# GAT softmax denominators: found per edge by segmented scans, and the all-ones product of the first gather pass removed

## The reference

```python
alpha = leaky_relu(a_src[src] + a_dst[dst] + a_edge, 0.2)
amax  = segment_max(alpha, dst)
ex    = exp(alpha - amax[dst])
denom = segment_sum(ex, dst)
w     = ex / (denom[dst] + 1e-16)
out   = segment_sum(h[src] * w[:, None], dst)   # h = x @ W, 128 wide
x     = x + out + bias
```

## Time and profile before

| | before |
|---|---|
| median of 3 runs | 6623.92 us |
| lowest and highest | 6615.25, 6627.57 us |
| span of the profiled execution (no other time is given for it) | 6635.5 us |
| PE, DVE, ACT, POOL busy | 74%, 41%, 17%, 52% |
| mean granted TensorE clock | 0.738 of full speed |
| first gather pass | from 403 to 1381 us of the span |

### The profile page before, as it was taken

One profiled execution on the slowest core, in us unless ns is written; L12 is line 12 of the kernel. 1 busy time (PEld: TensorE's weight loads), 2 busy tenths in 40 slices (PEclk: granted clock), 3 DMA queues, 4 the chain that ended last, 5 costly groups with the idle time before them and its releaser, 6 DMA issues.

```text
span 6635.5 us, 123629 instructions
## 1 busy us (share of the span) xinstructions
PE 4909.3 (74%) x40104; PEld 3977.9 (60%) x40104; DVE 2748.4 (41%) x9007; ACT 1139.0 (17%) x2152; POOL 3474.9 (52%) x3162
## 2 busy tenths in 40 slices
PE   2457877766666665699999999788888888844444
PEld 1346666644444443699999877666665666633333
DVE  6776666667777776532323111222221222222222
ACT  1622222222222221110000133111111000000000
POOL 2136566658888886000000000577775777767777
PEclk6567677666666665799999999788886666655555
DMA  4462222235555655553333466444443444422222
GB/s 133 136 184 76 74 76 77 74 80 102 97 100 99 101 99 116 177 176 121 93 97 97 141 237 233 154 155 155 160 154 119 131 130 129 129 64 59 59 59 58
DMA packets 608943, 781.60 MB, mean 118 GB/s; under 512 B 89922, under 2 KB 506922, under 8 KB 597722
## 3 DMA queue, kind: packets, MB, share of 16 engines
q1 hardware_dynamic: 371644, 437.53, 20.8%
q0 software_dynamic: 190720, 287.00, 20.1%
q10 hardware_dynamic: 46224, 52.61, 2.3%
HBM read 533.32 MB, written 243.79 MB: 117 GB/s over the span
## 4 chain that ended last, share of the span: by engine, by line
PE 42%; issue 16%; POOL 15%; DMA 13%; DVE 9%; DVEq 2%; ACT 2%; SPq 0%; ACTq 0%; POOLq 0%
PE PS L2284 16%; POOL ring L863 12%; PE PS L2168 7%; PE PS L2142 4%; PE PS L2205 4%; DMA part<-ring,cur 3%; DMA ring<-tab_l3c,SRC 3%; POOL part L882 3%; DVE ACC_B L1617 2%; PE PS L2430 2%; DMA ring<-tab_l3a,SRC 2%; PE PS L2170 1%; PE PS L2226 1%; DMA SCR<-hi_d 1%; DMA ring<-tab_l3b,SRC 1%
## 5 line engine op out<-in xcount | busy, mean ns | idle before, releaser
L2168 PE MATMUL PS<-QSEL,ring 128*128 128x64 f32 x7500 | 1489.3, 344 | 693.9 <-DMA ring<-tab_l3c,SRC 338.0
L2168 PEld LDWEIGHTS PS<-QSEL,ring 128*128 128x128 f32 x7500 | 1363.3, 256 | 948.3 <-issue 488.4
L882 POOL DMA_INDIRECT part<-ring,cur x625 | 1012.2, 1619 | 247.4 <-issue 168.8
L863 POOL DMA_INDIRECT ring<-tab_l3a,SRC x625 | 598.9, 958 | 636.4 <-issue 617.2
L863 POOL DMA_INDIRECT ring<-tab_l,SRC x625 | 609.8, 976 | 574.5 <-PE PS L2171 404.7
L2142 PE MATMUL PS<-ACC_B 128*128 128x320 f16 x2568 | 619.9, 409 | 151.8 <-DVE ACC_B L1617 151.6
L863 POOL DMA_INDIRECT ring<-tab_l3b,SRC x625 | 599.7, 960 | 232.1 <-issue 223.3
L863 POOL DMA_INDIRECT ring<-tab_l3c,SRC x625 | 595.3, 952 | 216.1 <-issue 189.3
L2284 PE MATMUL PS<-ACC_A,X 128*128 128x128 f16 x6400 | 560.8, 221 | 70.8 <-DVE ring L1853 65.1
L901 POOL DMA_DIRECT2D more<-ring x3 | 2.9, 973 | 1124.0 <-ACT ring L1123 782.9
L2226 PE MATMUL PS<-SCR,SEL 128*32 128x128 f32 x1250 | 281.3, 408 | 408.8 <-DVE SCR L1692 366.9
(11 more groups left out here) (456 smaller groups left out, 6876.4 us busy)
## 6 DMA issues: line engine op xcount, KB each, us to landing
ACC_A<-pairs_d SPq DMA_DIRECT2D x120, 1280.0 KB
pairs_d<-ACC_B ACTq DMA_DIRECT2D x320, 160.0 KB
tab_l3a<-SCR SPq DMA_DIRECT2D x40, 1024.0 KB, 4.5
tab_l3b<-SCR SPq DMA_DIRECT2D x40, 1024.0 KB, 4.4
SCR<-in_src SPq DMA_DIRECT2D x125, 320.0 KB, 3.5
tab_l3c<-SCR SPq DMA_DIRECT2D x40, 512.0 KB, 3.1
SCR<-hi_d SPq DMA_DIRECT2D x125, 160.0 KB, 3.1
SCR<-part SPq DMA_DIRECT2D x50, 256.0 KB, 4.0
```

What stands on the lines that cost most here:

```text
L863: pool.indirect_dma_start(ring[:, slot, 0:width], None, tab[p][:, :], bass.IndirectOffsetOnAxis(SRC[:, t:t + 1], 0)).then_inc(sem(f"pair_i ...
L882: pool.indirect_dma_start(part_d[j][:, :], bass.IndirectOffsetOnAxis(cur[:, s:s + 1], 0), ring[:, s, 0:D], None, compute_op=ALU.add).then_ ...
L2168: ins = mm(PS[:, s, ch * QWIN:(ch + 1) * QWIN], ring[:, slot, ch * P:(ch + 1) * P], hot, start=e == 0 and ch == 0, stop=e == end, skip_gro ...
```

## The change

Two parts.

1. In the softmax stage, after the exponential, the same forward and backward segmented scans as for the maximum now find for every edge the sum of its destination's exponentials. Forward plus backward minus the edge itself plus 1e-16 is inverted and multiplied onto `alpha`, so that `WGT` holds the finished softmax weight. The cut arrays for multiply-add scans (`same_dst` and others) are made while ScalarE works. TensorE turns row ends and carries twice more.
2. In the first gather pass the product with the all-ones f32 matrix (L2170) goes, with its columns in PSUM and in `ACC_A`, the fill of that accumulator, and the division in the dense step, which becomes a copy.

```diff
@@ vector engine, softmax stage, after the maximum is subtracted
+            link(vec.tensor_scalar(same_dst, new_dst, 0.0, None, ALU.is_equal))
+            link(vec.tensor_scalar(same_dst_back, new_dst_back, 0.0, None, ALU.is_equal))
+            link(vec.tensor_scalar(joined[:, 1:RQ], cut_in[:, 1:RQ], 0.0, None, ALU.is_equal))
+            link(vec.tensor_scalar(pass_on, gate, 0.0, None, ALU.is_equal))
+            link(vec.tensor_scalar(pass_back, gate_back, 0.0, None, ALU.is_equal))
+            dve.wait_ge(sem("exp_out"), 1)
+            link(vec.tensor_copy(alpha_back, alpha[:, ::-1]))
+            link(vec.tensor_tensor_scan(peak, same_dst, alpha, 0.0, ALU.mult, ALU.add))
+            link(vec.tensor_tensor_scan(peak_back, same_dst_back, alpha_back, 0.0, ALU.mult, ALU.add))
+            dve.sem_inc(sem("handed"), 1)
+            link(vec.memset(left[:, 0:1], 0.0))
+            link(vec.memset(right[:, RQ - 1:RQ], 0.0))
+            dve.wait_ge(sem("turned"), TURNED["sums_tr"])
+            link(vec.tensor_tensor(left[:, 1:RQ], PS[0:1, 7, 0:RQ - 1], joined[:, 1:RQ], ALU.mult))
+            link(vec.tensor_tensor(right[:, 0:RQ - 1], PS[0:1, 7, P + 1:P + RQ], joined[:, 1:RQ], ALU.mult))
+            link(vec.tensor_copy(right_in, right[:, ::-1]))
+            link(vec.tensor_tensor_scan(carried, pass_on, left, 0.0, ALU.mult, ALU.add))
+            link(vec.tensor_tensor_scan(carried_back, pass_back, right_in, 0.0, ALU.mult, ALU.add))
+            link(vec.tensor_copy(right, carried_back[:, ::-1]))
+            dve.sem_inc(sem("handed"), 1)
+            dve.wait_ge(sem("turned"), TURNED["sum_carries_tr"])
+            link(vec.tensor_copy(carry, PS[0:RQ, 7, 2 * P:2 * P + 2]))
+            link(vec.tensor_tensor_scan(peak, same_dst, alpha, carry[:, 0:1], ALU.mult, ALU.add))
+            link(vec.tensor_tensor_scan(peak_back, same_dst_back, alpha_back, carry[:, 1:2], ALU.mult, ALU.add))
+            link(vec.tensor_copy(peak_turned, peak_back[:, ::-1]))
+            link(vec.tensor_tensor(peak, peak, alpha, ALU.subtract))
+            link(vec.scalar_tensor_tensor(peak, peak, 1e-16, peak_turned, ALU.add, ALU.add))
+            link(vec.reciprocal(peak, peak))
+            vec.tensor_tensor(alpha, alpha, peak, ALU.mult).then_inc(sem("handed"), 1)
@@ vector engine, first gather pass
-                            vec.tensor_tensor(v, v, PS[:, s, 2 * QWIN:3 * QWIN], ALU.add)
+                            vec.tensor_tensor(v, v, PS[:, s, QWIN:2 * QWIN], ALU.add)
...
-                    den = part_in[:, u, 1, :]
-                    vec.reciprocal(den, block_cols(ACC_A[:, 1, :], b)).then_inc(sem("mean_step"), 1)
-                    dve.wait_ge(sem("mean_step"), n * 3 + 1)
-                    vec.tensor_tensor(part_in[:, u, 0, :], block_cols(ACC_A[:, 0, :], b), den, ALU.mult).then_inc(sem("mean_step"), 2)
+                    vec.tensor_copy(part_in[:, u, 0, :], block_cols(ACC_A[:, 0, :], b)).then_inc(sem("summed_in"), 1)
@@ tensor engine
-            pe.wait_ge(sem("exp_out"), 1)
+            pe.wait_ge(sem("handed"), HANDED["row_sums"])
+            nc.tensor.transpose(PS[0:1, 7, 0:RQ], peak[:, ROW - 1:ROW], ident[0:RQ, 0:RQ])
+            nc.tensor.transpose(PS[0:1, 7, P:P + RQ], peak_back[:, ROW - 1:ROW], ident[0:RQ, 0:RQ]).then_inc(sem("turned"), 1)
+            pe.wait_ge(sem("handed"), HANDED["sum_carries"])
+            nc.tensor.transpose(PS[0:RQ, 7, 2 * P:2 * P + 1], carried, ident[0:1, 0:1])
+            nc.tensor.transpose(PS[0:RQ, 7, 2 * P + 1:2 * P + 2], right, ident[0:1, 0:1]).then_inc(sem("turned"), 1)
+            pe.wait_ge(sem("handed"), HANDED["weighted"])
...
-                        if c["ones"]:
-                            mm(PS[:, s, QWIN:2 * QWIN], ones[:, :], hot, start=False, stop=e == end, skip_group_check=True)
-                            ins = mm(PS[:, s, 2 * QWIN:3 * QWIN], ones_h[:, :], QHOT[:, s, e, :], start=False, stop=e == end, skip_group_check=True)
+                        if c["degrees"]:
+                            ins = mm(PS[:, s, QWIN:2 * QWIN], ones_h[:, :], QHOT[:, s, e, :], start=False, stop=e == end, skip_group_check=True)
@@ scalar engine
-            nc.scalar.copy(ACC_A[:, 1, :], tiny.to_broadcast([P, NP])).then_inc(sem("exp_out"), 1)
```

More of the change, by code:

```diff
@@ L237, in edge_row @@
             return MULTI[0:1, 5 * TP + 64 + P * k:5 * TP + 64 + P * k + RQ]
-        first_dst, last_dst, cut_in, cut_row, gate, gate_back, left, right, right_in, carried, carried_back = (edge_row(k) for k in range(11))
+        first_dst, last_dst, cut_in, cut_row, gate, gate_back, left, right, right_in, carried, carried_back, joined, pass_on, pass_back = \
+            (edge_row(k) for k in range(14))
         relw = X[:, 0:4096]
@@ L322, in build @@
         more_d = [dram(f"more_{c}", (P, width * NP)) for width, c in CONVS]
[L326 to L329, removed]
+        PASS = {0: dict(F=D, wt=WGT, acc=ACC_A, degrees=True),
+                5: dict(F=HID, wt=WGT, acc=ACC_B, degrees=False),
+                6: dict(F=HID, wt=WGT, acc=ACC_A, degrees=False),
+                7: dict(F=D, wt=WGT, acc=ACC_B, degrees=False)}
         SPAN_STEPS = (3, 7, 11, 15)
         def chunks(p):
-            return 2 if PASS[p]["F"] == HID or PASS[p]["ones"] else 1
+            return PASS[p]["F"] // P
         def rows_of(v):
@@ L1636, in select @@
                         at = cols(QREL, g, QUAD).unsqueeze(2).to_broadcast([P, QUAD, QWIN])
-                        hot = QHOT if c["ones"] else QSEL
+                        hot = QHOT if c["degrees"] else QSEL
                         vec.tensor_tensor(hot[:, s, :, :], there, at, ALU.is_equal).then_inc(sem("s_hot"), 1)
@@ L1789, in l1_dense @@
                     block_scale(n)
-            dve.wait_ge(sem("exp_out"), 4)
+            dve.wait_ge(sem("exp_out"), 3)
             sums(0, l1_dense)
```

11 lines of the change are left out of this document (5 added, 6 removed).

## The result

The changed kernel takes 6451.09 us (median of 4 runs, 6446.48 to 6452.9), the kernel before 6625.74 us beside it (4 runs, 6615.25 to 6638.39): ratio 0.9735, 95% interval 0.9721 to 0.9749, 2.65% faster. The forecast was 6554 us, with a range of 6485 to 6610.

What follows compares the result with a forecast made beforehand. It took a loop through TensorE, VectorE and ScalarE to bound the first gather pass. Profiled: 6635.5 - 88 (pass) - 1 (tail) + 18.6 (scans) = 6565 us; the 70 us difference carried to the median gave 6554, range 6485 to 6610.

Steps and rivals of the forecast that it cites:

- stretch a of the pair: First 14.50 us of two first-gather-pass turns, including the loop's end; removed product saves 1.7 us at slow clock, 0 at fast.
- the 5.21 us at the loop's end: VectorE's "issue" stop at the end of the first gather pass's two-turn loop body, 5.21 us before the change.
- The scans: New softmax-stage work on the path from the logits to the first gather product: 18.6 us added, bounds 17 to 20.
- the shorter code: Sign in the first gather pass: the prediction is wrong if the loop-end stop of 5.21 us changes with the shorter code.
- The work in the pass: Removed product and division in the first gather pass: 5.4 us a pair of turns, 105 us gained (62 to 135).
- TensorE's wait for the tiles: Sign in the first gather pass: TensorE's wait for VectorE's one-hot tiles (L1617) grows above 131 us.
- The clock: TensorE's granted clock in the first gather pass falls from 0.70 to 0.64 (0.58 to 0.72), costing 17 us.
- Rival 1: TensorE's clock in the first gather pass falls to 0.5; 29 us net gain, 6595 us in all; chance 0.20.
- Rival 2: Clock rises to 0.85 or 0.89; first gather pass down to GpSimd's 790 us; 6492 or 6455 us; chance 0.20.
- Rivals 3 and 4: Third: TensorE's saving returns as tile wait, 6642 us, chance 0.06; fourth: little change, within 13 us, chance 0.06.
- the tail of the pass: Three blocks after the first gather pass's last turn lose one exposed reciprocal: 1 us gained.
- the stage behind it: Sign: stages after the first gather pass keep their lengths within 5 us.

Runs made afterwards that it cites:

- pad3: The changed kernel with three one-element fills added per VectorE turn, giving its loop body the old length: 6475.91 us, ratio 0.9763.
- product_kept: The changed kernel with the all-ones product still made, into PSUM columns that nothing reads: 6480.45 us, ratio 0.9767.
- both_kept_again: The changed kernel with the all-ones product put back, and a reciprocal and multiply in place of the copy, on chip 13: 7103.48 us, ratio 0.9946.

## Why the prediction was wrong

- **The step that failed** is stretch a of the pair: the 5.21 us at the loop's end was carried into the forecast unchanged, as a cost of the loop and not of where its code lies. The scans' code, costed at 18.6 us and nothing else, moved the loop body by 27 instructions and took the stop away: from 5.2 to 1.65 us at each return, 79.1 us of the pass in the changed kernel (865.7 to 786.6). The forecast named the stop among what would make it wrong, but by "the shorter code"; pad3 showed that the length alone was not it. It gave the stop's end no rival and no chance.
- **The scans**: 18.6 us expected, 18.6 measured, with the reciprocal at 4.15 us as in the earlier trace rows.
- **The work in the pass**: 105 us expected ahead of the clock's term, 110.5 measured with the stop in place. The total held; the steps by stretch were not measured one by one. With the stop in place its signs came too: TensorE's wait for the tiles 179.6 us from 455 to 1300 (above 131 was forecast) and GpSimd's for TensorE 80.6 (under 100).
- **The clock**: 0.64 expected, between 0.58 and 0.72, at a cost of 17 us. With the stop in place it stayed at 0.70 with TensorE busy 68% (592.74 of 865.7), so no fall came and the 17 us should not have been taken off. With the stop gone the removed work did lower it, from 0.78 to 0.74 (from 0.82 in product_kept), but the end of the stop had raised it more, and at GpSimd's rate the fall cost nothing that shows. The Trainium skill (TensorE: Matmul & The Clock Gate, "HAM oscillation") has matmul bursts between waits fall back at each wait. The runs agree with it in direction only with the stop gone, and the clock rose when TensorE's wait for the tiles fell with the stop (187.6 to 63.5 us in the pass). Rival 1's 0.5 was nowhere near.
- **Rival 2** named the end state, the pass on GpSimd's 790 us and 6455 us in all, but by a clock of 0.85 to 0.89. It was reached at 0.74. Its chance of 0.20 was set with the other cost in the loop taken as fixed.
- **Rivals 3 and 4** fell: in the kernel as measured TensorE's wait for VectorE's tiles went down (57.6 us from 455 to 1300, against 131.3), not up, and GpSimd's wait for TensorE went to 7, far below the 100 named.
- **The rest**: the tail of the pass 1.4 us shorter, 1 expected; the stage behind it 12.9 us shorter, where 5 was the bound, without a cause shown.

## What to carry to other kernels

An "issue" stop of several us that always stands at a loop's end need not be a property of the work: count the instruction queue's packets in that stretch of the DMA view, and if they grow with the returns of the loop, a few idle instructions ahead of it are worth trying before any change of the work. The word "issue" alone is no sign of it: on chip 13 VectorE's reciprocal (L1803) stood behind "issue" waits of up to 8.1 us in both_kept_again, with 12 packets in the pass. Code added in one stage can so change another stage that it does not touch; a forecast should give each such stop a case in which it vanishes, and one in which it appears. Where two gains lead to the same floor they don't add: here 115.8 and 110.5 us, each alone, gave 189.6 together.

## What the runs showed of the hardware

- VectorE's loop of 278 instructions stood 4.5 to 5.7 us at its longest stop, with 98 instruction packets in the pass, when it began at 555, 568 or 684 of its list, and at most 2.6 us, with 12 or 13 packets, at 579 or 582 (pad3). A loop of 272 stopped (6.9 us) at 700, and not at 582, 642 or 688, nor one of 274 at 582. Blocks of 128 instructions, of which three fit and four do not, account for all of these; a packet of 8.2 KB (0.80 MB by 98) is 128 times 64 bytes. How many blocks VectorE keeps was not measured, nor why five packets come at each return when the body touches four blocks.
- The Trainium skill (Runtime: NRT & Kernel Launch, "Instruction fetch mechanics") says that a taken branch whose target is not among the pages held makes the engine wait for a fetch by DMA. The runs agree in kind. It gives pages of 256 instructions; in the runs a shift of 129 instructions leaves the stop as it is, and one of 24 takes it away, which fits 128 and not 256.
- On three of the five numbered chips the same programs took 7.1% to 9.4% longer (before 7093 to 7146 against 6626, changed 7057 against 6451), with the changed pass at 972 instead of 787 us. GpSimd's gathers there stand in part behind waits of up to 3.0 us put down to "remote", 129.7 us of them in that pass, which the traces from the faster chips don't have. The cause was not looked for.
